# A fused attention and FP4 feed-forward block on one core: last batch's scaling moved to VectorE, ten unread matmul pairs fewer, another order of work

## The chip, the core and the metric

The kernel runs on one core of a Trainium2 chip. The time is device microseconds of one execution. The core has four compute engines, each of which works through its own instructions in the order in which they are written: PE (TensorE, matmuls and transposes), DVE (VectorE), ACT (ScalarE) and POOL (GpSimd). SP (SyncE) issues DMAs, and so does ACT. Engines wait for each other through semaphores.

## What is computed

For x of 8 batches x 512 rows x 128 columns, with xn = layernorm(x), the result is x + attention(xn) + ffn(xn):

```
qkv = xn @ w_qkv.T; q, k: 16 heads x 2 codes through fc_code; q = softmax over the codes
k_exp = exp(k - max over t); kv = cumsum(k_exp * v) / (cumsum(k_exp) + 1e-9)
attention = (sum over codes of q * kv) @ w_out.T

fp4(a): blocks of 16: scale = max|a| / 6, a / scale to the nearest of
        0, .5, 1, 1.5, 2, 3, 4, 6 (with sign), times scale
gate = fp4(xn) @ fp4(w_gate).T; up = fp4(xn) @ fp4(w_up).T      (352 columns each)
h = silu(gate) * up
ffn = fp4(h) @ fp4(w_down).T
```

All products are in fp32.

## The kernel before

A batch is 128 partitions x 4 tiles of 128 columns (a partition holds rows 4p to 4p+3, one in each tile). For each batch, the names in the code follow the work:

- DVE takes statistics (`stats`), ACT forms `xn`; PE transposes it (`xn_t` after ACT's copy) and multiplies by `wqkv_t` into `at_ps`. ACT copies `q_rel` and `v_sb`. DVE takes `k_max`, PE transposes it, DVE forms `k_negmax`, PE adds it, ACT writes the exponent into `kv`.
- POOL multiplies `kv<-v_sb,kv` (128x1024) and adds tile to tile (three `kv<-kv`, 128x288). PE sums over the partitions (`at_ps<-kv,before`), ACT adds the exponent of q (`at_ps<-q_rel`), DVE forms `kv<-kv,at_ps` (128x1152) and `den`, ACT its logarithm and exponent, DVE `den_p`, `den_r`, `q_n`. POOL forms `o_codes`, PE transposes and sums the codes, ACT copies `o_t`.
- fp4 of xn: DVE block maxima (`x_abs`, `x_max`, `x_recip`), ACT `x_r`, POOL `yx` = xn / scale, ACT squares its coarse part into PSUM (`s_ps<-yx`), DVE two operations (`sx`, `qx`) that leave the grid value, POOL `xq` = grid value times scale; PE transposes into `g_ps`, ACT copies `xq_t`.
- PE forms gates (`g_ps`, `h_ps`) and ups (`u_ps`), ACT the SiLU (`silu`), DVE `h`, `h_max`, `h_recip`, ACT `h_r`, POOL `yh`, ACT `s_ps<-yh` for a tile, DVE `sh` and `qh` (bf16, in SBUF), POOL `hq` = qh times h_max. PE transposes `hq`, ACT copies `hq_t`, PE sums the output product (`wo_t`) and the down products (`wd_t`) in `o_ps`, DVE adds x into `out_sb`, SP stores it.

There is one `s_ps` bank for yx and the four yh tiles, so that a new square waits for the DVE operation that read the last one. ACT needs two tables a batch, one with exponent and logarithm and one with SiLU, and loads each for 1.28 us.

The order on each engine is written out by hand: each engine's function is a loop over steps in which each piece of work stands under its own offset (`b = step - 55`) or fixed step, and the pieces of one step run in the order in which they are written. Batch 0 and batch 7 have pieces of their own. In batch 7, the four tiles of h go singly: POOL `yh` at L583, L357, L505, L386, DVE `sh` and `qh`, POOL `hq` at L362 (tile 0), L568 (1), L475 (3), L519 (2), and the output products in four banks (`o_ps`, `h_ps`, and both halves of `at_ps`) with one add each (L1098, L1406, L1400, L1208).

Among PE's work are 30 unread pairs: `o_ps<-before,ident`, two products of two constants that nobody reads.

## Time and profile before

| | us |
|---|---|
| median of 3 runs | 137.80 |
| lowest, highest | 137.77, 138.46 |
| the profiled execution | 137.86 |
| its span, from the first to the last instruction | 136.0 |
| PE, DVE, ACT, POOL busy in it | 129.3, 120.2, 114.4, 119.7 |

A row of a timeline gives the start and duration of an instruction, its engine and line, what it writes and reads, and, in brackets, how long its engine sat idle before it and what ended that. Durations overlap the next start by about 0.1 us, so sums go from start to start. Matmul ends are modelled. A row of windows gives the stretch, its length, for PE, its weight loads (PEld), DVE, ACT and POOL the busy time and (x count), then the granted clock of PE (1.00 is 2.4 GHz), the DMA share and GB/s.

### The profile page before, as it was taken

How to read it: one execution, taken by the hardware profiler on the slowest of the kernel's cores; microseconds unless marked ns; L12 is line 12 of the kernel's file. 1: busy time of each engine (PE TensorE's matmuls, PEld its weight loads, DVE VectorE, ACT ScalarE, POOL GpSimd, SP SyncE). 2: the span in 40 equal slices, each digit the busy share in tenths (PEclk: the TensorE clock that was granted, in tenths of full speed). 3: DMA queues.
4: the chain of work that ended last, by engine and by line, in shares of the span. 5: the costliest groups of instructions: out<-in, count | busy, mean ns of one | idle time of the engine just before them, and what ended most of it. 6: DMA issues, size and time to landing. Idle time of an engine off the chain costs nothing.

```text
span 136.0 us, 2542 instructions
## 1 busy us (share of the span) xinstructions
PE 129.3 (95%) x861; PEld 110.2 (81%) x861; DVE 120.2 (88%) x289; ACT 114.4 (84%) x280; POOL 119.7 (88%) x122
## 2 busy tenths in 40 slices
PE   2989999999999999999999999999999999978992
PEld 2979886888798878987898889788978895857992
DVE  1589999989999899989998999899989897999831
ACT  0778999979998999999899989998999778785640
POOL 5439889699999999999999999999999999999920
PEclk9999999999999999999999999999999999999999
DMA  4991000000000001000100020002000100010012
GB/s 104 317 367 65 5 2 0 2 0 2 0 5 0 0 0 77 5 0 0 77 0 5 2 80 0 0 0 82 0 0 0 77 0 0 5 77 0 6 71 77
DMA packets 4075, 5.14 MB, mean 38 GB/s; under 512 B 544, under 2 KB 2144, under 8 KB 4064
## 3 DMA queue, kind: packets, MB, share of 16 engines
q1 hardware_dynamic: 3088, 4.49, 9.4%
q10 hardware_dynamic: 976, 0.51, 1.3%
q8 instruction: 6, 0.10, 0.3%
q14 instruction: 5, 0.04, 0.1%
HBM read 2.90 MB, written 2.10 MB: 37 GB/s over the span
## 4 chain that ended last, share of the span: by engine, by line
PE 34%; ACT 21%; DVE 19%; POOL 19%; issue 4%; POOLq 0%; ACTq 0%
ACT L1025 4%; POOL o_codes L494 3%; DVE h_max L1358 2%; POOL hq L404 2%; POOL hq L529 2%; POOL yh L467 2%; PE at_ps L2040 2%; DVE h_max L1103 2%; ACT s_ps L1021 2%; ACT xn_t L922 2%; POOL kv L397 1%; POOL kv L449 1%; DVE sh L1300 1%; ACT silu L1025 1%; DVE x_abs L1174 1%
## 5 line engine op out<-in xcount | busy, mean ns | idle before, releaser
L494 POOL TENSOR_TENSOR o_codes<-kv,q_n 128x1024 f32<-128x1024 f32 x6 | 11.8, 1972 | 0.0
L449 POOL TENSOR_TENSOR kv<-v_sb,kv 128x1024 f32<-128x1024 f32 x6 | 11.8, 1969 | 0.0
L664 ACT ACTIVATE xn<-x_all,shift,rstd 128x128 f32<-128x128 f32 x24 | 9.9, 489 | 0.0
L2040 PEld LDWEIGHTS at_ps<-wqkv_t,xn_t 128*128 128x128 f32 x48 | 8.1, 190 | 1.3
L404 POOL TENSOR_TENSOR hq<-qh,h_max 128x704 f32<-128x704 bf16 x6 | 8.3, 1385 | 0.9 <-DVE qh L1363 0.9
L2040 PE MATMUL at_ps<-wqkv_t,xn_t 128*128 128x192 f32 x48 | 8.8, 326 | 0.0
L378 POOL TENSOR_TENSOR yh<-h,h_r 128x704 f32<-128x704 f32 x6 | 8.3, 1388 | 0.3 <-ACT h_r L793 0.3
L467 POOL TENSOR_TENSOR yh<-h,h_r 128x704 f32<-128x704 f32 x6 | 8.3, 1386 | 0.0
L529 POOL TENSOR_TENSOR hq<-qh,h_max 128x704 f32<-128x704 bf16 x6 | 8.3, 1383 | 0.0
L1392 DVE TENSOR_TENSOR kv<-kv,at_ps 128x1152 f32<-128x1152 f32 x6 | 8.1, 1344 | 0.0
L726 ACT ACT_TABLE_LOAD x6 | 7.7, 1283 | 0.1
L1025 ACT ACT_TABLE_LOAD x6 | 7.7, 1283 | 0.1
L442 POOL TENSOR_TENSOR yx<-xn,x_r 128x512 f32<-128x512 f32 x6 | 6.4, 1060 | 0.3 <-ACT x_r L846 0.3
L537 POOL TENSOR_TENSOR xq<-qx,x_max 128x512 f32<-128x512 bf16 x6 | 6.3, 1054 | 0.0
L1738 PE MATMUL at_ps<-ident,o_codes 128*128 128x128 f32 x24 | 5.6, 273 | 0.0
L1739 PE MATMUL at_ps<-ident,o_codes 128*128 128x128 f32 x24 | 5.6, 273 | 0.0
L1103 DVE TENSOR_REDUCE h_max<-h 128x44 f32<-128x748 f32 x6 | 5.5, 922 | 0.0
L1358 DVE TENSOR_REDUCE h_max<-h 128x44 f32<-128x748 f32 x6 | 5.5, 922 | 0.0
L810 ACT ACTIVATE o_t<-at_ps 128x512 f32<-128x512 f32 x6 | 3.6, 598 | 2.1 <-PE at_ps L1739 2.1
L367 POOL TENSOR_TENSOR kv<-kv 128x288 f32<-128x288 f32 x6 | 4.8, 801 | 0.3
L2163 PE MATMUL o_ps<-wd_t,hq_t 128*128 128x128 f32 x36 | 5.0, 275 | 0.0
L1903 PE MATMUL o_ps<-wd_t,hq_t 128*128 128x128 f32 x36 | 5.0, 275 | 0.0
(517 smaller groups left out, 525.7 us busy)
## 6 DMA issues: line engine op xcount, KB each, us to landing
x_all<-x SPq DMA_DIRECT2D x8, 256.0 KB, 4.9
out<-out_sb SPq DMA_DIRECT2D x7, 256.0 KB, 2.0
out<-out_sb SPq DMA_DIRECT2D x2, 128.0 KB, 1.7
w_raw<-w_down ACTq DMA_DIRECT2D x1, 176.0 KB, 4.8
wqk_raw<-w_qkv ACTq DMA_DIRECT2D x1, 128.0 KB, 3.5
w_raw<-w_gate SPq DMA_DIRECT2D x1, 128.0 KB, 3.2
w_raw<-w_up ACTq DMA_DIRECT2D x1, 128.0 KB, 3.5
wqkv_t<-w_qkv ACTq DMA_DIRECT2D x1, 64.0 KB, 4.3
```

The lines of the kernel that those rows point to most:

```text
L378: nc.gpsimd.tensor_tensor(blocks(yh[:, p, 0 * FF:2 * FF], PAIR * HB), h[:, p, 0 * HB:2 * HB, 0:BLOCK], spread(h_r[:, p, 0 * HB:2 * HB], PA ...
L404: nc.gpsimd.tensor_tensor(hq[:, 4 * p + 2:4 * p + 4, 0:FF].rearrange("p t (b k) -> p t b k", k=BLOCK), qh[:, p, 2 * FF:4 * FF].rearrange(" ...
L449: nc.gpsimd.tensor_tensor(kv[:, p, :, 0:KV].rearrange("p j (c h w) -> p j c h w", c=CODE, w=HEAD), v_sb[:, p, :].rearrange("p (j h w) -> p ...
L467: nc.gpsimd.tensor_tensor(blocks(yh[:, p, 2 * FF:4 * FF], PAIR * HB), h[:, p, 2 * HB:4 * HB, 0:BLOCK], spread(h_r[:, p, 2 * HB:4 * HB], PA ...
L494: nc.gpsimd.tensor_tensor(o_codes[:, p, :, :].rearrange("p j (c w) -> p j c w", w=HEAD), kv[:, p, :, 0:KV].rearrange("p j (c w) -> p j c w ...
L529: nc.gpsimd.tensor_tensor(hq[:, 4 * p + 0:4 * p + 2, 0:FF].rearrange("p t (b k) -> p t b k", k=BLOCK), qh[:, p, 0 * FF:2 * FF].rearrange(" ...
L664: last = nc.scalar.activation(xn[:, p, j * D:(j + 1) * D], x_all[:, b, j * D:(j + 1) * D], ACT.Identity, bias=shift[:, b, j:j + 1], scale= ...
L1025: nc.scalar.activation(silu[:, 1, :], h_ps[:, 0:FF], ACT.Silu).then_inc(silu1_done, 1)
L1103: nc.vector.tensor_reduce(h_max[:, p, 0 * HB:2 * HB], h[:, p, 0 * HB:2 * HB, :], AX.X, ALU.max, apply_absolute_value=True).then_inc(hmax0_ ...
L1358: nc.vector.tensor_reduce(h_max[:, p, 2 * HB:4 * HB], h[:, p, 2 * HB:4 * HB, :], AX.X, ALU.max, apply_absolute_value=True).then_inc(hmax1_ ...
L1392: nc.vector.tensor_tensor(kv[:, p, :, :], kv[:, p, :, :], a_ps[:, 0:ROW].unsqueeze(1).broadcast_to([P, TILES, ROW]), ALU.add).then_inc(bad ...
L2040: last = nc.tensor.matmul(at_ps[:, j // 2, j % 2 * QKV:(j % 2 + 1) * QKV], xn_t[:, p, j * P:(j + 1) * P], wqkv_t[:, :], start=(j % 2 == 0) ...
```

## The change

It changes six things.

1. hq of the last batch. The second rounding step writes the grid value as fp32 back into the PSUM bank from which it read instead of bf16 into `qh`, and DVE multiplies from there into `hq`. Tiles 1, 2 and 3 of that batch use the banks `g_ps`, `u_ps0` and `u_ps1` instead of `s_ps`. Four POOL instructions are gone. Batch 0's and the middle batches' hq stay on POOL, two tiles at a time.
2. Unread pairs: 20 instead of 30.
3. Loads: both pieces of w_up head ACT's queue (one was third there, one fourth on SP's), w_down is before the value weights.
4. The last batch is stored in four DMAs of one tile, in the order 0, 3, 1, 2, rather than two.
5. In the last batch PE starts the output product (`wo_t`) of each tile in a piece of its own.
6. All engines' pieces stand under other steps and in another order, and some waits change with it.

```diff
 sp (loads)
-            sp.dma_start(w_raw[0:FF - 2 * P, FFP + 2 * P:2 * FFP], w_up[2 * P:FF, :]).then_inc(gu_in, 16)
 act (loads, as they now stand)
+            act.dma_start(w_raw[:, FFP:FFP + 2 * P].rearrange("p (c k) -> p c k", c=2),
+                          w_up[0:2 * P, :].rearrange("(c p) k -> p c k", p=P)).then_inc(gu_in, 16)
+            act.dma_start(w_raw[0:FF - 2 * P, FFP + 2 * P:2 * FFP], w_up[2 * P:FF, :]).then_inc(gu_in, 16)
             act.dma_start(code_sb[:, :], code_t).then_inc(codes_in, 16)
             act.dma_start(wqk_raw[:, :, :], w_qkv[0:2 * D, :].rearrange("(s p) k -> p s k", p=P)).then_inc(codes_in, 16)
             act.dma_start(w_raw[:, 2 * FFP:], w_down).then_inc(down_in, 16)
             act.dma_start(wqkv_t[:, 2 * HC:], w_qkv[2 * D:3 * D, :]).then_inc(wv_in, 16)
 pool (one of four, all for b = BATCHES - 1)
-                    nc.gpsimd.tensor_tensor(blocks(hq[:, 4 * p + 0, 0:FF], HB), blocks(qh[:, p, 0 * FF:1 * FF], HB), spread(h_max[:, p, 0 * HB:1 * HB], HB), ALU.mult).then_inc(hq0_done, 1)
 dve (tile 0; the other tiles alike, from g_ps, u_ps0, u_ps1)
+                    nc.vector.scalar_tensor_tensor(out=s_ps[:, 0:FF], in0=s_ps[:, 0:FF], scalar=OFFSET, in1=sh[:, p, 0 * FF:1 * FF], op0=ALU.add, op1=ALU.subtract).then_inc(qh0_done, 1)
+                    dve.wait_ge(qh0_done, 8)
+                    nc.vector.tensor_tensor(blocks(hq[:, 4 * p + 0, 0:FF], HB), blocks(s_ps[:, 0:FF], HB), spread(h_max[:, p, 0 * HB:1 * HB], HB), ALU.mult).then_inc(hqz0_done, 1)
 act (tile 2; tiles 1 and 3 alike)
+                    nc.scalar.activation(u_ps[0][:, 0:FF], coarse(yh[:, p, 2 * FF:3 * FF]), ACT.Square, scale=SLOPE).then_inc(sqh2_done, 1)
 pe (ten of thirty such pieces are gone)
-                    for _ in range(2):
-                        nc.tensor.matmul(o_ps[:, 0:P], ident[:, :], before[:, :], start=True, stop=True)
 pe (last batch, tile 0; before, one piece)
+                    pe.wait_ge(ot_done, 8)
+                    pe.wait_ge(resid_done, 7)
+                    nc.tensor.matmul(o_ps[:, 0 * P:1 * P], o_t[:, p, 0 * P:1 * P], wo_t[:, :], start=True, stop=False).then_inc(woz0_done, 1)
 sp (last batch)
-            for half in range(2):
-                for ready in ((residz0_done, residz1_done), (residz2_done, residz3_done))[half]:
-                    sp.wait_ge(ready, 1)
-                sp.dma_start(out_v[b][:, half * 2 * P:(half + 1) * 2 * P], out_sb[:, b % 2, half * 2 * P:(half + 1) * 2 * P]).then_inc(last_stored, 16)
+            for j, ready in ((0, residz0_done), (3, residz3_done), (1, residz1_done), (2, residz2_done)):
+                sp.wait_ge(ready, 1)
+                sp.dma_start(out_v[b][:, j * P:(j + 1) * P], out_sb[:, b % 2, j * P:(j + 1) * P]).then_inc(last_stored, 16)
```

PE in the opening, around the transposes of xn of batch 2 (`at_ps<-ident,xn`), before. The rows of `o_ps<-before,ident` are unread pairs.

```order
L1706 MATMUL h_ps<-ident,w_dq 128x128 x3
L1710 MATMUL o_ps<-before,ident 128x128 x2
L1724 MATMUL g_ps<-ident,xq 128x128 x4
L1814 MATMUL at_ps<-kv,before 128x288
L1824 MATMUL o_ps<-before,ident 128x128 x2
L1827 MATMUL o_ps<-before,ident 128x128 x2
L1830 MATMUL o_ps<-before,ident 128x128 x2
L1833 MATMUL o_ps<-before,ident 128x128 x2
L1911 MATMUL at_ps<-ident,xn 128x128 x4
```

The same place now:

```order
L2144 MATMUL g_ps<-ident,xq 128x128 x4
L1706 MATMUL at_ps<-kv,before 128x288
L1740 MATMUL u_ps<-wu_t,xq_t 128x352
L1774 MATMUL h_ps<-ident,w_dq 128x128 x3
L1784 MATMUL at_ps<-ident,xn 128x128 x4
L1877 MATMUL u_ps<-wu_t,xq_t 128x352
L1890 MATMUL g_ps<-wg_t,xq_t 128x352
```

The four pairs ahead of the transposes are gone; an up product and the transposes of the down weights stand there.

DVE in a middle period, from x_abs to the large kv, before:

```order
L1174 TENSOR_REDUCE x_abs<-xn 128x32
L1202 TENSOR_REDUCE x_max<-x_abs 128x32
L1243 TENSOR_TENSOR h<-silu,u_ps 128x22x16
L1259 TENSOR_TENSOR h<-silu,u_ps 128x22x16
L1281 RECIPROCAL x_recip<-x_max 128x32
L1300 SCALAR_TENSOR_TENSOR sh<-s_ps,yh 128x352
L1358 TENSOR_REDUCE h_max<-h 128x44
L1363 SCALAR_TENSOR_TENSOR qh<-s_ps,sh 128x352
L1390 TENSOR_REDUCE at_ps<-at_ps 128x64
L1392 TENSOR_TENSOR kv<-kv,at_ps 128x1152
```

Now, with `out_sb` of the batch before among them (it was ahead of the first row, or behind it, before):

```order
L1447 TENSOR_REDUCE x_abs<-xn 128x32
L1490 TENSOR_TENSOR h<-silu,u_ps 128x22x16
L1515 SCALAR_TENSOR_TENSOR sh<-s_ps,yh 128x352
L1551 TENSOR_TENSOR out_sb<-x_all,o_ps 128x512
L1556 SCALAR_TENSOR_TENSOR qh<-s_ps,sh 128x352
L1562 TENSOR_REDUCE x_max<-x_abs 128x32
L1597 TENSOR_TENSOR h<-silu,u_ps 128x22x16
L1607 RECIPROCAL x_recip<-x_max 128x32
L1617 TENSOR_REDUCE h_max<-h 128x44
L1080 TENSOR_REDUCE at_ps<-at_ps 128x64
L1099 TENSOR_TENSOR kv<-kv,at_ps 128x1152
```

sh and qh moved ahead of the second h and of h_max.

DVE at the end, from the last batch's q_n to the last hq, before:

```order
L1588 SCALAR_TENSOR_TENSOR q_n<-at_ps,den_r 128x128
L1591 SCALAR_TENSOR_TENSOR sh<-s_ps,yh 128x352
L1606 TENSOR_TENSOR h<-silu,u_ps 128x22x16
L1620 SCALAR_TENSOR_TENSOR qh<-s_ps,sh 128x352
L1622 TENSOR_REDUCE h_max<-h 128x22
L1624 RECIPROCAL h_recip<-h_max 128x22
L1071 SCALAR_TENSOR_TENSOR sh<-s_ps,yh 128x352
L1088 SCALAR_TENSOR_TENSOR qh<-s_ps,sh 128x352
L1184 TENSOR_TENSOR out_sb<-x_all,o_ps 128x512
L1131 SCALAR_TENSOR_TENSOR sh<-s_ps,yh 128x352
L1352 SCALAR_TENSOR_TENSOR qh<-s_ps,sh 128x352
```

Now, from the first round in place on:

```order
L1197 SCALAR_TENSOR_TENSOR s_ps<-s_ps,sh 128x352
L1255 SCALAR_TENSOR_TENSOR sh<-u_ps,yh 128x352
L1291 RECIPROCAL h_recip<-h_max 128x22
L1352 TENSOR_TENSOR hq<-s_ps,h_max 128x352
L1437 SCALAR_TENSOR_TENSOR u_ps<-u_ps,sh 128x352
L1510 SCALAR_TENSOR_TENSOR sh<-g_ps,yh 128x352
L1520 TENSOR_TENSOR hq<-u_ps,h_max 128x352
L1530 TENSOR_TENSOR out_sb<-x_all,o_ps 128x512
L1612 SCALAR_TENSOR_TENSOR g_ps<-g_ps,sh 128x352
L1381 SCALAR_TENSOR_TENSOR sh<-u_ps,yh 128x352
L1456 TENSOR_TENSOR hq<-g_ps,h_max 128x352
L1466 SCALAR_TENSOR_TENSOR u_ps<-u_ps,sh 128x352
```

One product more (tile 2) follows. POOL's four products are gone, and its last instruction is yh of tile 2, behind o_codes.

## Rows read from the trace of the kernel before

**Rows 1.** The page: busy time of each engine, and TensorE's clock by slices.

```profile
PE 129.3 (95%) x861; PEld 110.2 (81%) x861; DVE 120.2 (88%) x289; ACT 114.4 (84%) x280; POOL 119.7 (88%) x122
...
PEclk9999999999999999999999999999999999999999
```

**Rows 2.** Windows of one period: length, busy time of each engine, clock, DMA share.

```profile
73.91:82.39 8.48, 8.48 (x60) 7.20 (x59) 8.48 (x21) 7.97 (x21) 8.25 (x9) 1.00 0.09 33
82.39:87.77 5.38, 5.38 (x35) 4.54 (x34) 4.91 (x13) 5.30 (x12) 5.38 (x4) 1.00 0.00 0
sum 13.86, PE 13.86 PEld 11.74 DVE 13.38 ACT 13.27 POOL 13.63; mean PE 6.93 PEld 5.87 DVE 6.69 ACT 6.63 POOL 6.81
```

**Rows 3.** Timeline of DVE in that period: start, duration, engine, line, operation.

```profile
84.74 0.53 DVE L1462 SCALAR_TENSOR_TENSOR qh<-s_ps,sh 128x352 bf16<-128x352 f32 x1
...
87.77 0.52 DVE L1561 TENSOR_TENSOR h<-silu,u_ps 128x352 f32<-128x352 f32 x1 [0.34 <-ACT silu L1025]
```

**Rows 4.** Timeline of ACT in that period.

```profile
85.98 1.28 ACT L1025 ACT_TABLE_LOAD   x1
87.27 0.46 ACT L1025 ACTIVATE silu<-h_ps 128x352 f32<-128x352 f32 x1
```

**Rows 5.** Timeline of PE in the opening: three unread pairs, batch 2's transposes.

```profile
2.44 1.22 PE L1642 MATMUL o_ps<-before,ident 128*128 128x128 f32 x4 [2.44 <-POOL head_of L348]
...
6.34 0.61 PE L1669 MATMUL o_ps<-before,ident 128*128 128x128 f32 x4
...
26.54 0.61 PE L1824 MATMUL o_ps<-before,ident 128*128 128x128 f32 x4
...
28.32 0.60 PE L1911 MATMUL at_ps<-ident,xn 128*128 128x128 f32 x4
```

**Rows 6.** Timeline of ACT in the opening.

```profile
6.55 1.65 ACT L633 ACTIVATE xn<-x_all,shift,rstd 128x128 f32<-128x128 f32 x4 [0.38 <-POOL shift L430]
8.79 0.24 ACT L705 ACTIVATE w_r<-w_recip 128x48 f32<-128x48 f32 x1 [0.60 <-DVE w_recip L1177]
...
28.96 0.60 ACT L922 ACTIVATE xn_t<-at_ps 128x512 f32<-128x512 f32 x1 [0.66 <-PE at_ps L1911]
```

**Rows 7.** Timeline of DVE in the opening.

```profile
6.03 0.95 DVE L1515 TENSOR_REDUCE w_abs<-w_raw 128x48 f32<-128x768 f32 x1 [1.04 <-DMA w_raw<-w_up]
...
30.23 0.29 DVE L1466 TENSOR_TENSOR den_p<-at_ps,den 128x128 f32<-128x128 f32 x1 [0.46 <-ACT at_ps L967]
...
32.52 0.52 DVE L1561 TENSOR_TENSOR h<-silu,u_ps 128x352 f32<-128x352 f32 x1
...
38.64 0.53 DVE L1273 SCALAR_TENSOR_TENSOR sh<-s_ps,yh 128x352 f32<-128x352 f32 x1 [0.26 <-ACT s_ps L762]
...
46.13 0.52 DVE L1561 TENSOR_TENSOR h<-silu,u_ps 128x352 f32<-128x352 f32 x1 [0.33 <-ACT silu L1025]
```

**Rows 8.** Timeline of DVE from the last steady period to q_n of the last batch.

```profile
101.76 0.52 DVE L1561 TENSOR_TENSOR h<-silu,u_ps 128x352 f32<-128x352 f32 x1 [0.27 <-ACT silu L1025]
...
120.86 1.34 DVE L1385 TENSOR_TENSOR kv<-kv,at_ps 128x1152 f32<-128x1152 f32 x1
...
124.16 0.29 DVE L1588 SCALAR_TENSOR_TENSOR q_n<-at_ps,den_r 128x128 f32<-128x128 f32 x1
```

**Rows 9.** Timeline of POOL at the end.

```profile
123.98 0.78 POOL L362 TENSOR_TENSOR hq<-qh,h_max 128x352 f32<-128x352 bf16 x1
...
124.72 1.97 POOL L573 TENSOR_TENSOR o_codes<-kv,q_n 128x1024 f32<-128x1024 f32 x1
```

**Rows 10.** Timeline of all engines over the last operations.

```profile
129.88 0.78 POOL L519 TENSOR_TENSOR hq<-qh,h_max 128x352 f32<-128x352 bf16 x1 [0.95 <-DVE qh L1352]
...
133.53 0.29 DVE L1208 TENSOR_TENSOR out_sb<-x_all,at_ps 128x128 f32<-128x128 f32 x1 [0.60 <-PE at_ps L1755]
```

**Rows 11.** The page's DMA issues: size, us from issue to landing.

```profile
out<-out_sb SPq DMA_DIRECT2D x7, 256.0 KB, 2.0
out<-out_sb SPq DMA_DIRECT2D x2, 128.0 KB, 1.7
```

## What the change does to the time

> **What bounds the kernel now.** I read the busy row of the page first: TensorE, ScalarE, VectorE and GpSimd are all busy 84% to 95% of a 136.0 us span [rows 1], so no share names the limit. The timelines of the four engines show three parts: an opening (to 46.13, where VectorE forms the first h of batch 2), a steady part of four periods (46.13 to 101.76), and an end (to 133.82, the last add on VectorE). One period runs 13.86 us, during which VectorE is busy 13.38, ScalarE 13.27, GpSimd 13.63, TensorE all of it [rows 2].
>
> What sets the period is a loop of two engines. From h L1561 (73.91) to kv L1392 (82.39) VectorE is busy 8.48 of 8.48 us. From kv it goes through h_recip, den, sh to qh L1462 at 84.74 [rows 2, 3]; then ScalarE may write the square of the next yx into s_ps (0.6), loads the SiLU table (85.98, 1.28) and forms silu (87.27, 0.46), for which VectorE waits 0.34 us at 87.77 [rows 3, 4]. 8.48 + 5.38 = 13.86. GpSimd and TensorE have only 0.2 us of slack each and follow.
>
> In the opening, TensorE never rests: unread pairs (ident times before, written to o_ps and never read) fill it. Four stand ahead of the transposes of batch 2's xn: 26.54 to 28.32, 1.78 us [rows 5]. ScalarE waits 0.66 for those transposes (xn_t at 28.96) [rows 6], den_log and its exponent come behind xn_t on ScalarE, VectorE waits 0.46 for them at den_p, and the next h comes at 32.52 [rows 7]. In the end, batch 7's four hq tiles are scaled on GpSimd, the last at 129.88 after a wait of 0.95 for VectorE's qh; from there transposes, copy, product and add run to 133.82 [rows 9, 10].
>
> **The change, part by part.** The diff's name speaks of the first and last batch; the orders show the four GpSimd products moved for the last batch only (batch 0 keeps its two double ones). So I count one batch.
>
> Opening, first weights. w_abs waits for w_up until 6.03 [rows 7]. Both w_up pieces now head ScalarE's queue and the last piece needed is w_gate's second, one issue (0.5 us) ahead of the old last one, so I take 5.5. w_recip no longer stands behind w_down's maxima, so w_r comes near 7.0 rather than 8.79 [rows 6]. But xn of batch 0, four activations of 1.65 us that began at 6.55, now stands behind w_r: 0.6 later, while the codes' four small activations stand behind xn. Behind the weights VectorE gets free earlier by 0.4 to 0.7. Six issues instead of five on ScalarE put its first table load 0.45 later, which ends before the statistics' results are missed by more than 0.1. I let these cancel: zero, between +0.6 and -0.7.
>
> Opening, pairs. Of 30 unread pairs 20 remain, and the four ahead of batch 2's transposes and one behind are gone. Where they stood TensorE has an up product, batch w_down's transposes: 0.59 + 0.33. The 0.66 that ScalarE waited goes, and the den chain, the s_ps write, the table load and h of batch 1 all move by it: 32.52 becomes about 31.9. The next period has the same VectorE work with one wait of 0.26 at sh L1273 [rows 7], which goes because that write of s_ps no longer follows the k exponent closely, and about 0.1 in small gaps. So h of batch 2 comes at 46.13 - 1.0 = 45.1. Bounds: 0.2 (another engine, GpSimd with its 2 us k-v product ahead of yx, becomes late) and 1.7 (the first batch's SiLU work, which I place 2 us earlier, carries through).
>
> Four periods. VectorE's instructions between kv and the next h are the same ones in the same order, and between h and kv the same set in another order (out_sb and one sh move behind the first of the two h, h_max last). So the loop's two pieces remain 8.48 and 5.38. Walking the new order by the durations of the period, the third s_ps write, now ahead of the exp table load, is ready 0.2 us before VectorE wants it, the exponent of q for at_ps 0.6 before, and GpSimd ends its list 0.3 before the next release. 4 x 13.86 = 55.44 against 55.63 measured (46.13 to 101.76; the last of the four had 13.99) [rows 7, 8]: -0.2. Bounds -1.0 (down to the roughly 13.65 that TensorE's issue times add up to) and +2 (a half microsecond per period).
>
> Turn to the last batch, 101.76 to q_n's end at 124.45 [rows 8], 22.7 us. GpSimd has kv's last prefix adds ahead of hq and of the big o_codes of batch 6 instead of behind it, 1.93 earlier in its list, and ScalarE's table load comes sooner. VectorE's list between is the same but for h of tile 2 (0.43), which goes ahead of q_n in place of the last round of tile 0 (0.43), which goes behind. By VectorE's sum the second kv comes 18.6 us after the h rather than 19.1 [rows 8], q_n with it: -0.5, between 0 and -1.0. GpSimd would be ready for o_codes by then because hq of tile 0 (0.78, 123.98) no longer stands before it (124.72) [rows 9].
>
> Last stretch, q_n's end to the last add's end: 9.37 now. VectorE now has behind q_n: h_max 0.45, four rounds, three sh and four products, eleven at about 0.43 start to start, a reciprocal 0.2, out_sb 0.6, together 6.0 us; with 0.3 for operations that follow their own input directly, the last hq ends 6.3 after q_n. On that last path stand then transposes 0.5, copy 0.5, three products 0.9 and add 0.3, with handovers 2.4: 8.7, so -0.7. The GpSimd product of 0.78 with its handovers on the old path is what goes. The in-place round in PSUM and the product read from PSUM into hq do not exist in the trace. Lower bound: the 0.43 of every 352-column VectorE operation that reads PSUM; upper: the 0.78 of the same product on GpSimd [rows 9, 10], which times four plus four gives 2.8 us more. I take 0.43, since the operand count and shape are those of qh at 84.74 (0.53 with its overlap) [rows 3], and keep -1.2 to +1.5 for the term.
>
> Stores. Four of 64 KB instead of two of 128; the last still starts after the last add, and landing took 1.7 us for 128 KB against 2.0 for 256 KB [rows 11]. I take 0, between -0.2 and +0.4 (the third issue, about 0.4, still running). The Trainium skill, DMA: Bandwidth & Descriptors, section on where the time of a DMA goes, has a fixed part of about 2 us plus bytes over 436 GB/s; by it the halves would save about 0.15 us, an estimate that the sum doesn't hold.
>
> Sum: -1.0 - 0.2 - 0.5 - 0.7 = -2.4. The profiled execution took 137.86 us, its span of 136.0 and 1.86 around it; the median of the runs shown is 137.8, so I predict **135.4**.
>
> **Rivals.**
> 1. The opening's gain is lost: GpSimd's or ScalarE's new order in the first 30 us replaces the removed wait. For it: xn held behind w_r, and yx of batch 1 now behind the 1.97 us k-v product. Then only 1.2 remains: 136.6.
> 2. The periods shrink to about 13.65: TensorE's and GpSimd's own work. For it, the relief of ScalarE ahead of its table load; against, the write of s_ps still waits for the same qh. 135.4 - 1.0 = 134.4.
> 3. VectorE becomes the bound of the end: each of the eight new or changed PSUM operations costs 0.15 more, or out_sb of batch 6 holds o_ps's product: 136.6.
> 4. Slower: ScalarE misses a date in every period. The s_ps write (0.4) that moved ahead of the exp table load delays the k exponent, the prefix sum on TensorE, the q exponent and so VectorE's kv. With the 0.6 of slack that I find, a delay of 1.0 us makes each period 0.4 longer, and six of them eat the 2.4: the point from which it decides. At 1.1 the price is 6 x 0.5 = 3.0 and the result 138.4.
> 5. The clock. The first pair took 1.22 us, that at 6.34 0.61, four matmuls each [rows 5]; the page's clock row reads 9, its highest, in all 40 slices, the end included, where TensorE waits several times [rows 1]. Fewer pairs leave gaps near 11 and 14 us; I count none over 0.8 us. Ten microseconds of opening at half the clock would cost about 3 with TensorE as the bound: 138.5.
>
> For the last the Trainium skill (TensorE: Matmul & The Clock Gate, the table of what to do) warns of idle gaps between bursts of matmuls and would have the clock fall to 1.2 GHz, which speaks against taking pairs out. What it would give here is rival 5's time.
>
> **How the numbers follow.** Forecast 0.52 (its own range 134.7 to 136.3), rival 1 0.14, rival 2 0.11, rival 3 0.09, rival 4 0.08, rival 5 0.03, and 0.03 for gains and losses that cancel. The range 134.0 to 137.0 reaches the first three rivals and leaves out the slower ones. A change of 0.5% (0.7 us) is about what a measurement of this kernel can tell from none. Faster by more: forecast and rivals 1 to 3 with most of their spread, 0.84; within, 0.08; slower, 0.08.
>
> **What would show it.** h L1309 of batch 2 near 45.1 with no wait of ScalarE for xn's transposes; periods of 13.86 with VectorE full between h L1309 and kv L1099; the second kv of the end 18.6 after batch 6's h; 352-column operations in PSUM of 0.52 us, 0.43 apart; GpSimd idle after about 126; 2.1 to 2.3 us from the last add to the end. Periods over 14.2, a clock below 1.00 in the first 40 us, or PSUM products of 0.7 would prove me wrong.

## The result and the profile after

| | before | after |
|---|---|---|
| median, us (10 runs each, same chip) | 138.09 | 136.86 |
| lowest, highest | 137.23, 139.85 | 136.46, 137.55 |
| ratio of the times, 95% interval | | 0.9923 [0.9897, 0.9949] |
| the profiled execution, its span | 137.86, 136.0 | 136.56, 134.5 |

The change makes the kernel 1.2 us faster (0.8%). Forecast were 2.4 us and 135.4. Before's median is 0.3 above that of the three runs which the prediction started from, so the time missed by 1.5 us and the difference by 1.2. The range and the sign held. In all tables the medians are of all runs, and the ratios leave out those in a slower state, more than 1.5% above the fastest run of the same kernel.

The page of the kernel after; the first line answers to [rows 1], the other to [rows 11] (size, median us from issue to landing):

```profile
PE 125.9 (94%) x821; PEld 106.4 (79%) x821; DVE 121.8 (91%) x293; ACT 114.0 (85%) x280; POOL 116.5 (87%) x118
...
out<-out_sb SPq DMA_DIRECT2D x4, 64.0 KB, 1.6
```

VectorE timeline of after, opening; answers to [rows 7] (line numbers are those of the new kernel):

```profile
4.89 0.95 DVE L1144 TENSOR_REDUCE w_abs<-w_raw 128x48 f32<-128x768 f32 x1 [0.47 <-DMA w_raw<-w_gate]
...
8.39 0.77 DVE L1338 BATCH_NORM_STATS2 stats<-x_all 128x6 f32<-128x256 f32 x2 [0.37 <-DMA x_all<-x]
...
10.94 0.54 DVE L1342 SCALAR_TENSOR_TENSOR w_s<-g_ps,w_y 128x384 f32<-128x384 f32 x1
...
20.26 0.52 DVE L1222 TENSOR_TENSOR h<-silu,u_ps 128x352 f32<-128x352 f32 x1 [0.25 <-PE u_ps L1815]
...
24.48 0.69 DVE L1447 TENSOR_REDUCE x_abs<-xn 128x32 f32<-128x512 f32 x1 [0.55 <-ACT xn L653]
...
30.61 0.29 DVE L1250 TENSOR_TENSOR den_p<-at_ps,den 128x128 f32<-128x128 f32 x1 [0.25 <-ACT at_ps L990]
...
32.90 0.52 DVE L1309 TENSOR_TENSOR h<-silu,u_ps 128x352 f32<-128x352 f32 x1 [0.28 <-ACT silu L1044]
...
46.02 0.52 DVE L1309 TENSOR_TENSOR h<-silu,u_ps 128x352 f32<-128x352 f32 x1 [0.30 <-ACT silu L1044]
```

w_abs comes 1.14 earlier than in [rows 7], yet h of batch 1 comes at 32.90, 0.38 later. (A second profile of the same kernel, e0_changed_again below, has it at 33.58, so the profile after is an early one.) ScalarE's rows, against [rows 6]: w_r comes 2.1 earlier; the wait for batch 2's transposes ahead of xn_t is gone, but xn_t itself is no earlier, and the wait now stands at den_log:

```profile
6.66 0.24 ACT L721 ACTIVATE w_r<-w_recip 128x48 f32<-128x48 f32 x1 [1.27 <-DVE w_recip L1294]
...
29.06 0.59 ACT L949 ACTIVATE xn_t<-at_ps 128x512 f32<-128x512 f32 x1
...
29.95 0.31 ACT L966 ACTIVATE den_log<-den 128x128 f32<-128x128 f32 x1 [0.30 <-DVE den L1165]
```

Windows of the same period as in [rows 2]: stretch, length, busy time (and count) of PE, PEld, DVE, ACT, POOL, clock, DMA share, GB/s.

```profile
73.59:81.98 8.39, 8.39 (x60) 7.12 (x59) 8.39 (x21) 8.02 (x21) 8.15 (x8) 1.00 0.09 33
81.98:87.35 5.37, 5.37 (x35) 4.57 (x34) 4.90 (x13) 5.31 (x12) 5.37 (x5) 1.00 0.01 3
```

VectorE from the last steady period to the end; answers to [rows 8] and [rows 10]:

```profile
101.05 0.52 DVE L1309 TENSOR_TENSOR h<-silu,u_ps 128x352 f32<-128x352 f32 x1 [0.28 <-ACT silu L1044]
...
120.27 1.34 DVE L1585 TENSOR_TENSOR kv<-kv,at_ps 128x1152 f32<-128x1152 f32 x1
...
123.44 0.29 DVE L1104 SCALAR_TENSOR_TENSOR q_n<-at_ps,den_r 128x128 f32<-128x128 f32 x1
...
128.28 0.51 DVE L1456 TENSOR_TENSOR hq<-g_ps,h_max 128x352 f32<-128x352 f32 x1
128.71 0.52 DVE L1466 SCALAR_TENSOR_TENSOR u_ps<-u_ps,sh 128x352 f32<-128x352 f32 x1
129.27 0.53 DVE L1622 TENSOR_TENSOR hq<-u_ps,h_max 128x352 f32<-128x352 f32 x1
...
132.14 0.29 DVE L1366 TENSOR_TENSOR out_sb<-x_all,at_ps 128x128 f32<-128x128 f32 x1 [0.38 <-PE at_ps L2151]
```

Start to start, the two executions compare so:

| stretch | before | after | difference | forecast |
|---|---|---|---|---|
| start to h of batch 1 | 32.52 | 32.90 | +0.38 | -0.6 |
| to h of batch 2 | 13.61 | 13.12 | -0.49 | -0.4 |
| four periods | 55.63 | 55.03 | -0.60 | -0.2 |
| h of batch 6 to q_n's end | 22.69 | 22.68 | -0.01 | -0.5 |
| q_n's end to the last add's end | 9.37 | 8.70 | -0.67 | -0.7 |
| last add to the span's end | 2.18 | 2.07 | -0.11 | 0 |
| sum, the span | 136.0 | 134.5 | -1.50 | -2.4 |

The time fell by 1.30, since what lies around the span was 2.06 instead of 1.86.

### The profile page after: what moved, and what is told of

It is laid out like the page before. It is cut to its first block, busy times and chain, and to the rows that moved or that the text cites. A ratio compares the mean times of both kernels' runs of the same rounds, so it can differ in the third digit from the quotient of the medians.

```text
span 134.5 us, 2464 instructions
## 1 busy us (share of the span) xinstructions
PE 125.9 (94%) x821; PEld 106.4 (79%) x821; DVE 121.8 (91%) x293; ACT 114.0 (85%) x280; POOL 116.5 (87%) x118
## 4 chain that ended last, share of the span: by engine, by line
PE 78%; ACT 10%; DVE 4%; POOL 4%; issue 2%; POOLq 0%
PE at_ps L1910 5%; PE o_ps L2131 3%; PE o_ps L2115 3%; PE o_ps L1951 3%; PE o_ps L1842 2%; PE u_ps L2136 2%; ACT xn L653 2%; PE u_ps L1877 2%; PE u_ps L2021 2%; PE h_ps L2056 2%; PE h_ps L1901 2%; PE g_ps L2032 2%; PE g_ps L1890 2%; PE at_ps L1696 2%; PE at_ps L1719 2%; PE at_ps L1720 2%
## 5 line engine op out<-in xcount | busy, mean ns | idle before, releaser
L2115 PE MATMUL o_ps<-wd_t,hq_t 128*128 128x128 f32 x36 | 5.0, 275 | 0.0
L1842 PE MATMUL o_ps<-wd_t,hq_t 128*128 128x128 f32 x36 | 5.0, 275 | 0.0
L1951 PE MATMUL o_ps<-wd_t,hq_t 128*128 128x128 f32 x36 | 5.0, 275 | 0.0
L2131 PE MATMUL o_ps<-wd_t,hq_t 128*128 128x128 f32 x36 | 5.0, 275 | 0.0
```

What stands on the lines that cost most here:

```text
L1951: last = nc.tensor.matmul(o_ps[:, 0 * P:1 * P], hq_t[:, 0, c * P:(c + 1) * P], wd_t[:, c * P:(c + 1) * P], start=False, stop=(c == CHUNKS ...
L2115: last = nc.tensor.matmul(o_ps[:, 2 * P:3 * P], hq_t[:, 2, c * P:(c + 1) * P], wd_t[:, c * P:(c + 1) * P], start=False, stop=(c == CHUNKS ...
L2131: last = nc.tensor.matmul(o_ps[:, 3 * P:4 * P], hq_t[:, 3, c * P:(c + 1) * P], wd_t[:, c * P:(c + 1) * P], start=False, stop=(c == CHUNKS ...
```

## The experiments

"h1" is the start of h of batch 1 on VectorE, "w_s" that of the first w_s (rounding of the gate and up weights). Each ratio is against runs of before on the same chip, whose median there was 138.1 to 138.6. Each profile had a granted clock of 1.00, but for e1_pool_swap's. The numbers w_s, h1 and span are of one execution each.

| run | median (lowest to highest) | ratio [95%] | w_s | h1 | w_s to h1 | span |
|---|---|---|---|---|---|---|
| before | 138.09 (137.23, 139.85) | | 11.69 | 32.52 | 20.83 | 136.0 |
| after | 136.86 (136.46, 137.55) | .9923 [.9897, .9949] | 10.94 | 32.90 | 21.96 | 134.5 |
| e1_pool_swap | 136.88 | .9858 [.9777, .9938] | | | | |
| e2_xpath | 136.49 (136.34, 136.86) | .9845 [.9777, .9913] | 10.74 | 32.71 | 21.97 | 134.3 |
| e4_qkv_path | 136.94 (136.92, 137.04) | .9875 [.9809, .9941] | 11.40 | 33.26 | 21.86 | 134.9 |
| e5_both | 136.86 (136.32, 136.98) | .987 [.9791, .995] | 10.75 | 32.65 | 21.90 | 134.3 |
| e3_before_4pairs_out | 137.78 (137.39, 138.41) | .9943 [.9907, .9978] | 11.60 | 32.27 | 20.67 | 135.6 |
| e6_loads_as_before | 137.57 (136.91, 139.73) | .9939 [.9898, .9981] | 12.61 | 34.66 | 22.05 | 136.3 |
| e7_both_2pairs_out | 137.17 (136.71, 137.62) | .988 [.98, .9959] | 12.07 | 33.97 | 21.90 | 135.6 |
| e8_hq_on_gpsimd | 137.81 (137.18, 138.36) | .9935 [.9903, .9967] | 11.21 | 33.18 | 21.97 | 135.5 |
| e12_hq_two_each | 137.31 (136.74, 139.07) | .9913 [.9881, .9945] | 11.54 | 33.49 | 21.95 | 135.1 |
| e14_hmax_order | 138.46 (137.87, 138.99) | 1.0003 [.9976, 1.0029] | 11.27 | 33.24 | 21.97 | 136.4 |
| e9a_attention0_first | 137.16 (136.91, 137.71) | .9923 [.9894, .9951] | 11.46 | 33.41 | 21.95 | 135.0 |
| e9_attention01_first | 137.77 (137.0, 139.3) | .9973 [.9939, 1.0007] | 10.99 | 33.36 | 22.37 | 134.9 |
| e0_changed_again | 137.06 (136.81, 137.45) | .9898 [.9871, .9925] | 11.62 | 33.58 | 21.96 | 135.2 |
| e2r_xpath_again | 136.92 (136.3, 137.09) | .9876 [.9844, .9907] | 11.32 | 33.29 | 21.97 | 134.9 |
| e16_xn0_in_the_wait | 136.72 (136.4, 136.88) | .9869 [.9844, .9895] | 11.35 | 33.31 | 21.96 | 134.9 |
| e17a_codes_behind_wy | 137.21 (136.47, 137.84) | .992 [.9887, .9952] | 11.57 | 33.52 | 21.95 | 135.1 |
| e17_codes_and_xpath | 136.98 (136.68, 137.55) | .9916 [.9887, .9946] | 11.12 | 33.29 | 22.17 | 134.9 |
| e18_batch2_stats_later | 136.82 (136.62, 137.37) | .9884 [.984, .9928] | 11.55 | 33.50 | 21.95 | 135.1 |

Two columns tell most of the story. In the changed kernel and in all versions of it w_s to h1 is 21.86 to 22.37, in 13 of 17 profiles 21.90 to 21.97, against 20.83 before; and span less h1 is 101.5 to 101.7 wherever the end and the periods were left alone. So a profile's span is that of its first w_s plus a constant, and no reordering that I made between w_s and h1 shortened that stretch by more than 0.10.

### The opening: what holds h of batch 1

**GpSimd's order.** First suspicion: yx of batch 1 behind the 1.97 us product of k and v. Changed kernel, yx put ahead of it:

```diff
 pool (yx of the middle batches)
-                if 1 <= b < BATCHES - 1:
+                if 2 <= b < BATCHES - 1:
 pool (ahead of kv<-v_sb,kv of batch 0)
+                    b = 1
+                    pool.wait_ge(xr_done, b + 1)
+                    nc.gpsimd.tensor_tensor(blocks(yx[:, p, :], TILES * XB), blocks(xn[:, p, :], TILES * XB), spread(x_r[:, p, :], TILES * XB), ALU.mult).then_inc(yx_done, 1)
```

> The changed kernel with one edit: on GpSimd, yx of batch 1 stands ahead of the k-v product of batch 0 instead of behind it. Theory A (GpSimd's order lost the opening: 1.97 us of k-v product ahead of yx): yx starts about 17.8 instead of 19.68, ScalarE's wait of 0.36 goes, h of batch 1 comes at 32.3 to 32.5 instead of 32.90, time 136.4. Theory B (x_r of batch 1 only ends at 19.57, because VectorE takes x_abs of batch 1 behind two statistics and ScalarE x_r behind the table load): yx still starts at 19.6, GpSimd waits for it, the k-v product comes at 20.6 instead of 17.76 and all that follows on GpSimd up to 2.9 later less the slack; h of batch 1 33.0 to 34.0, time 137.0 to 137.9.

The profiled execution ran at a granted clock of 0.86 and took 149.5 us, so only the order of its early events is read. GpSimd's timeline:

```profile
20.32 1.06 POOL L501 TENSOR_TENSOR yx<-xn,x_r 128x512 f32<-128x512 f32 x1 [2.28 <-ACT x_r L852]
```

GpSimd stands idle before yx for x_r of ScalarE, so it isn't the product that holds yx. Its other three executions took 136.4 to 136.9, as the changed kernel: the theory fell.

**The two paths of batch 1.** e2 puts x_abs, x_max and x_recip of batch 1 ahead of two statistics on VectorE, x_r ahead of ScalarE's table load and yx ahead of the product; e4 puts the transposes, xn_t, its product, q_rel and v_sb of batch 1 earlier; e5 does both.

```diff
 dve (e2; ahead of the statistics of two later batches)
+                    b = 1
+                    dve.wait_ge(xn_done, b + 1)
+                    nc.vector.tensor_reduce(x_abs[:, :, 0], blocks(xn[:, p, :], TILES * XB), AX.X, ALU.max, apply_absolute_value=True).then_inc(xabs_done, 1)
...
 act (e2; ahead of the silu of batch 0)
+                    nc.scalar.activation(x_r[:, p, :], x_recip[:, p, :], ACT.Copy, scale=GRID_MAX / SHADE).then_inc(xr_done, 1)
 pe (e4; the transposes of batch 1, in place of an unread pair, and two waits for the silu)
-                if 1 <= b < BATCHES - 1:
+                if 2 <= b < BATCHES - 1:
...
+                    pe.wait_ge(silu1_done, 1)
...
+                        pe.wait_ge(silu2_done, 1)
```

> The changed kernel with batch 1's fp4 path put as in the kernel before: on VectorE x_abs, x_max and x_recip ahead of the two statistics at 16.25 and 16.92, on ScalarE x_r ahead of the SiLU table load, on GpSimd yx ahead of the k-v product. Theory B: yx starts at 17.8, the wait of 0.36 before s_ps<-yx goes, xn of batch 2 and the exp table load come 0.4 earlier, h of batch 1 at 32.5, time 136.4. Theory C (the order on TensorE binds: q_rel waits for the product of batch 1's xn_t, L1910 at 20.65, whatever yx does): the 0.36 comes back as a longer wait before q_rel (0.4 becomes about 0.8), xn of batch 2 stays at 22.8, h of batch 1 at 32.8 to 33.0, time 136.8 to 137.0.

> The changed kernel with batch 1's attention path earlier: on TensorE the transposes of xn ahead of the up and gate products of batch 0 and the xn_t product ahead of gate 2 of batch 0, on ScalarE xn_t ahead of the second silu, q_rel and v_sb ahead of the third; two waits of TensorE for a silu that this order needs. Theory C: the wait of 0.40 before q_rel goes, q_rel starts at 21.4 and xn of batch 2 at 22.4 instead of 22.81, exp table load 24.5, h of batch 1 at 32.5, time 136.4. Theory B (yx alone binds, s_ps<-yx at 20.77 stays): xn of batch 2 within 0.15 of 22.8, h of batch 1 at 32.8 to 33.0.

> The edits of the two kernels before this one together (batch 1's fp4 path and its attention path earlier). If both waits of ScalarE, 0.36 and 0.40, made the loss: xn of batch 2 at 22.0 to 22.2, exp table load at 24.2 to 24.3, the large kv of batch 1 at 27.2, h of batch 1 at 32.2, time 136.1. If VectorE's or GpSimd's own work takes over (theory D: the statistics moved behind and the k-v product 1.0 later make the prefix sum or x_recip late), h of batch 1 stays at 32.8 or later although both waits are gone.

In e2 yx of batch 1 starts at 17.70 instead of 19.68, and the wait of 0.36 for it is gone, but ScalarE then waits 0.84 instead of 0.40 at q_rel, and w_s to h1 is the same 21.97. In e4, where ScalarE still waits 0.36 and 0.34, it is 21.86, in e5, with one wait of 0.81 at q_rel, 21.90: 0.1 at most. None of the three differs from the changed kernel by more than the intervals leave open.

**Unread pairs.** Before with only the four pairs of step 70 taken out:

```diff
 pe (before; four such pieces)
-                if step == 70:
-                    for _ in range(2):
-                        nc.tensor.matmul(o_ps[:, 0:P], ident[:, :], before[:, :], start=True, stop=True)
```

> The kernel before with one edit: the four unread pairs ahead of the transposes of batch 2's xn are gone (L1824 to L1833). The prediction's step: ScalarE's wait of 0.66 before xn_t goes whole, h of batch 1 at 31.9 instead of 32.52, and all after it 0.6 earlier: time 0.6 less than before. Rival (the cap): den on VectorE ends at 29.33 whatever TensorE does, den_log started at 29.58, so only 0.2 can be gained: ScalarE now waits 0.2 to 0.4 before den_log for den, h of batch 1 at 32.3, time 0.2 less than before. Rival (clock): the gap of 1.8 us brings TensorE's clock down, 1 us or more slower.

VectorE's timeline of it, against [rows 7], and then a row of ScalarE's:

```profile
27.25 1.34 DVE L1347 TENSOR_TENSOR kv<-kv,at_ps 128x1152 f32<-128x1152 f32 x1
...
29.98 0.29 DVE L1466 TENSOR_TENSOR den_p<-at_ps,den 128x128 f32<-128x128 f32 x1 [0.25 <-ACT at_ps L967]
...
32.27 0.52 DVE L1561 TENSOR_TENSOR h<-silu,u_ps 128x352 f32<-128x352 f32 x1
```

```profile
29.32 0.31 ACT L956 ACTIVATE den_log<-den 128x128 f32<-128x128 f32 x1 [0.46 <-DVE den L1440]
```

The four pairs delayed den_p by 0.25 (30.23 before), not by the 0.66 that ScalarE waited: behind the transposes the next late thing is `den`, which VectorE itself ends at 29.3 and for which ScalarE now waits 0.46 before its logarithm. VectorE's wait at den_p fell from 0.46 to 0.25 and stays there. From kv to h is 5.02, as in after (27.88 to 32.90), and 5.22 before: 0.20 of the 0.25 arise there, the other 0.05 stood already at kv. The time (137.78, 0.57 under before's) allows for a little more, with the next interval 0.17 shorter too (h of batch 2 at 45.71).

Whether the pairs that are left hold something was asked by taking two more out of e5:

```diff
 pe (the pairs that stand at L1893 and L1828 in the changed kernel)
-                    for _ in range(2):
-                        nc.tensor.matmul(o_ps[:, 0:P], ident[:, :], before[:, :], start=True, stop=True)
```

> The changed kernel with batch 1's fp4 and attention paths earlier, as in e5_both, and two unread pairs gone (L1893, L1828, one on each side of the transposes of xq of batch 0), 18 left. Theory F (TensorE is the bound from 15.5 to 22.1 and its unread pairs stand on the path): the first gate product 0.4 earlier (16.75), ScalarE's wait before q_rel 0.4 instead of 0.81, h of batch 1 at 32.2 to 32.3 instead of 32.65, time 0.4 less than e5_both. Theory E (the sum of ScalarE's work is the bound): the gain at q_rel is lost again by xn of batch 2, h of batch 1 within 0.1 of 32.65.

w_s to h1 is 21.90, exactly e5's. TensorE now waits 0.36 for xq, so these two pairs held nothing; ahead of the product of batch 2's xn_t it waits 1.61, and in the changed kernel 1.62 (32.07). ScalarE still waits 0.81 at q_rel for TensorE's product of batch 1's xn_t, so TensorE as a whole isn't cleared by this.

**Loads.** The changed kernel with before's order of loads:

```diff
 sp
+            sp.dma_start(w_raw[0:FF - 2 * P, FFP + 2 * P:2 * FFP], w_up[2 * P:FF, :]).then_inc(gu_in, 16)
 act (the first of the two loads of w_up is back behind wqk_raw, w_down behind wqkv_t)
-            act.dma_start(w_raw[0:FF - 2 * P, FFP + 2 * P:2 * FFP], w_up[2 * P:FF, :]).then_inc(gu_in, 16)
```

> The changed kernel with the loads issued as in the kernel before (second piece of w_up fourth on SP, the first third on ScalarE's queue, five issues on ScalarE). If the early weights carry the opening now: w_abs at 6.0 instead of 4.89, w_r at 7.8 instead of 6.66 with xn of batch 0 behind it, h of batch 0 at 20.6 instead of 19.49, h of batch 1 0.8 to 1.1 later, time 137.7. If they are worth nothing (the rest of the opening is bound by ScalarE's own work, which here starts 0.5 earlier): h of batch 1 within 0.3 of 32.9, time 136.9.

```profile
7.16 0.95 DVE L1144 TENSOR_REDUCE w_abs<-w_raw 128x48 f32<-128x768 f32 x1 [2.62 <-DMA w_raw<-w_up]
...
12.61 0.54 DVE L1342 SCALAR_TENSOR_TENSOR w_s<-g_ps,w_y 128x384 f32<-128x384 f32 x1
```

With before's order of loads w_s is 1.0 to 1.7 later than in the two profiles of the changed kernel, and the median is 0.5 to 0.7 higher. How much of that is the loads is less sure: in this execution w_abs waited for w_up until 7.16, 1.1 later than in before (6.03) with the same order of loads, the runs were on other chips, and by the ratios, whose intervals overlap, it is 0.2 to 0.6 us. The sign fits the first theory; my sum had put the term at nothing.

**Attention of batches 0 and 1 forward**, to fill ScalarE's waits ahead of its table loads (e9a: batch 0, e9: both; three and four unread pairs fewer):

```diff
 act (e9a; the k exponent of batch 0, until now behind the copies of the weights, ahead of wg_t; xn_t, q_rel, v_sb alike)
+                    act.wait_ge(kshift_done, 1)
...
                     act.wait_ge(wT_done, 1)
                     nc.scalar.activation(wg_t[:, :], h_ps[:, 0:FF], ACT.Copy, scale=GRID_MAX ** -2).then_inc(wev_done, 1)
 pe (e9a; the product that shifts k, and the transpose of k_max, earlier; three pairs out)
-                        nc.tensor.matmul(o_ps[:, 0:P], ident[:, :], before[:, :], start=True, stop=True)
```

> The changed kernel with batch 0's attention path put forward: three unread pairs ahead of xn's transposes gone (17 left), ScalarE's xn_t, q_rel and v_sb of batch 0 ahead of what filled the time before them, k_max and k_negmax earlier on VectorE, their products earlier on TensorE, the k exponent ahead of wg_t, the k-v product of batch 0 ahead of w_dq of the down weights. Theory H (the order of batch 0's attention path lost the opening): the k exponent of batch 0 at 15.7 instead of 17.40, but batch 1's path stands where it did, so h of batch 1 gains only what ScalarE no longer waits (0.2 to 0.4): 32.5 to 32.7. Theory D (GpSimd and VectorE pay for it: w_dq of the down weights, rstd and shift 1.9 later): h of batch 1 at 33 or later.

> The same, and batch 1's fp4 and attention paths follow it ahead of batch 0's SiLU work: x_abs, x_max, x_recip ahead of w_s of the down weights, x_r, xn_t of batch 1 ahead of the SiLU table load, TensorE's transposes and product of batch 1's xn ahead of the up products of batch 0, q_rel and v_sb ahead of the second silu; 16 unread pairs left. Theory E (what counts up to h of batch 1 is the sum of ScalarE's work and its waits, and all its waits behind 10 us, 1.7 us in the changed kernel, can be filled by this order): its waits between 10 and 32 fall to about 0.6, the exp table load of batch 1 at 24.0 instead of 24.94, h of batch 1 at 32.0 to 32.3, time 136.1. Theory F (TensorE's packed list between 15.5 and 22 is the bound): batch 0's gates and ups come 1.3 later, h of batch 1 at 32.9 or later.

ScalarE's timeline of e9:

```profile
24.79 0.24 ACT L674 ACTIVATE h_r<-h_recip 128x44 f32<-128x44 f32 x1 [0.79 <-DVE h_recip L1404]
```

The waits that were filled open again at h_r, which waits for VectorE. w_s to h1 became 22.37 in e9, and its time can't be told from before's; in e9a it stayed at 21.95. Neither moved h of batch 1 forward, so these theories fell as well.

**What starts it.** Two executions of the same program differed: w_s at 10.94 and at 11.62 (e0). e2 was run once more beside it (e2r).

> The changed kernel itself once more, on the chip of the two runs that follow, as their yardstick: 136.6 to 137.1; h of batch 1 at 32.7 to 33.2, since the loads of the opening land up to half a microsecond apart from one execution to the next.

> e2_xpath once more beside the changed kernel. If putting batch 1's fp4 path ahead is worth what its trace showed (h of batch 1 at 32.71 instead of 32.90): 0.2 less than the changed kernel. If its median of 136.5 was more than chance, 0.4 less. If nothing: the two medians within 0.1.

e2r is 0.14 under e0 in the median, with overlapping runs, so the low 136.49 of e2 did not come again. GpSimd's code_diff waits for wqk_raw, which now lands behind w_up, and w_y stands behind it: 7.30 in the one execution, 8.05 in the other, and h1 followed. Three runs took up what leads to w_y. e16 (on e2) has xn of batch 0 in ScalarE's wait for w_recip, xn_t of batch 0 earlier, three unread pairs out and a load moved to SP; e17a has code_diff behind w_y in the changed kernel, e17 the same in e2.

```diff
 pool (e17a, e17)
-                if step == 5:
+                if step == 7:
                     pool.wait_ge(codes_in, 2 * 16)
                     nc.gpsimd.tensor_tensor(code_diff[:, 0:1], code_sb[:, 1:2], code_sb[:, 0:1], ALU.subtract)
 act (e16; xn of batch 0, now ahead of w_r)
+                    act.wait_ge(shift_done, 1)
+                    for j in range(TILES):
+                        last = nc.scalar.activation(xn[:, p, j * D:(j + 1) * D], x_all[:, b, j * D:(j + 1) * D], ACT.Identity,
...
```

> e2_xpath, and ScalarE's wait of 1.27 for w_recip in the opening filled: the value weights' load issued on SP, so that ScalarE has five issues, xn of batch 0 ahead of w_r instead of behind it, three unread pairs ahead of xn's transposes gone (17 left), xn_t of batch 0 ahead of the first square of the weights. Theory E (ScalarE's work and waits up to h of batch 1 are the bound): xn at 6.0 to 6.2 and the wait gone, w_r at 7.8, the first square at 9.5 instead of 9.33 behind xn_t, the SiLU table load at 17.2 instead of 17.7, h of batch 1 at 32.2 to 32.3, time 0.4 less than e2_xpath. Theory W (the weights' own path, w_recip to w_r to w_y to w_dq to wg_t, carries the opening, and its 1.1 us of delay at w_r is what counts): the SiLU table load at 18.2 or later, h of batch 1 at 33.2 or later, time 0.5 or more above e2_xpath.

> The changed kernel with one edit on GpSimd: the two code_diff operations, which wait for the load of the q and k weights (wqk_raw), stand behind w_y of the gate and up weights instead of ahead of it. Theory W2 (w_up ahead of wqk_raw in the queue made GpSimd, not the weights, late: in twelve traces h of batch 1 comes 25.4 to 25.6 behind the start of w_y, and w_y starts when wqk_raw has landed, 0.4 to 1.5 behind w_r): w_y at 6.9 to 7.0 in every execution, h of batch 1 at 32.4 to 32.5, time 0.5 to 0.8 less than the changed kernel's 136.9 to 137.1. Rival (another wait takes its place: code_bd on ScalarE then waits for code_diff behind the 1.5 us of w_y, and the first square behind it): code_bd 0.3 or more later, the first square at 9.6 or later, h of batch 1 32.9 or later.

> The same edit on top of e2_xpath. Theory W2: h of batch 1 at 32.2 to 32.3, time 0.2 less than e17a_codes_behind_wy and 0.5 to 0.8 less than e2r_xpath_again's 136.9: 136.2. Rival as there: no gain over e2r_xpath_again.

In e16 w_r came at 7.76, 1.1 later than in after, and w_s to h1 stayed at 21.96 and the time at 136.72, so the time moved in neither of the ways expected; e17 gave no gain over e2r. VectorE's timeline of e17a:

```profile
7.47 0.76 DVE L1494 BATCH_NORM_STATS2 stats<-x_all 128x6 f32<-128x256 f32 x2 [0.62 <-DMA x_all<-x]
...
9.03 0.77 DVE L1338 BATCH_NORM_STATS2 stats<-x_all 128x6 f32<-128x256 f32 x2 [0.35 <-DMA x_all<-x]
```

w_y started at 7.21, earlier than in any other version with these loads but e2 and e5, and h1 still came at 33.52: w_y only came late together with what sets w_s. That is x. The statistics of batches 1 and 2 on VectorE wait for their loads, up to 0.97 and 0.42, ahead of the scales of w_down and of batch 0; with x on time they begin at 6.75 and 8.39, late at 7.5 and 9.1. From the statistics of batch 2 to the first w_s are 2.53 to 2.55 us in all profiles of the new order but e6 (2.78) and e18, and no row of VectorE in between shows a wait; in after the next is at 20.26.

**The last question** was whether VectorE's full list or the chain of batch 0's scales through x_r sets the start of what leads to h1.

```diff
 dve (statistics of batch 2, from ahead of x_abs of batch 0 to behind its x_recip)
+                if step == 2:
+                    dve.wait_ge(x_in[2], 16)
+                    for a in range(2):
+                        last = nc.vector.bn_stats(stats[:, 2, a, :], x_all[:, 2, a * 2 * D:(a + 1) * 2 * D].rearrange("p (two d) -> p d two", two=2))
+                    last.then_inc(stats_done, 1)
```

> The changed kernel with one thing moved on VectorE: the two statistics of batch 2 (0.68 from start to start, until now ahead of x_abs of batch 0, where they wait 0.35 to 0.37 for the load of x) stand behind x_recip of batch 0. Nothing is left out. In the profiles so far the statistics of batch 2 began at 8.39 (changed kernel) and 9.08 (its second profile), and h of batch 1 came 24.50 after them both times; the first x_r came at 10.77 and 11.45, and h of batch 1 came 22.13 after it both times. Theory V: from these statistics to 20.26 VectorE is packed, and its own list is the bound of the opening. Then the order inside it gives nothing, only the wait for x goes (0.37, and 0.4 of it comes back as a wait for xn ahead of x_abs): the first w_s stays at 10.9 to 11.1, sx at 12.8 to 13.0, h of batch 1 at 32.9 to 33.1, time 136.7 to 136.9. Theory R: the bound is the chain x_abs, x_max, x_recip, x_r, yx, s_ps of batch 0. Then x_abs begins at 8.5 to 8.7, x_r at 10.3 to 10.5, sx at 12.4 to 12.6, and h of batch 1 comes at 32.4 to 32.6; time 136.3 to 136.5. In both, a late load of x no longer moves h of batch 1.

x of batch 1 came later than ever (VectorE's timeline):

```profile
7.89 0.77 DVE L1494 BATCH_NORM_STATS2 stats<-x_all 128x6 f32<-128x256 f32 x2 [0.84 <-DMA x_all<-x]
...
11.55 0.54 DVE L1342 SCALAR_TENSOR_TENSOR w_s<-g_ps,w_y 128x384 f32<-128x384 f32 x1
...
33.50 0.52 DVE L1314 TENSOR_TENSOR h<-silu,u_ps 128x352 f32<-128x352 f32 x1 [0.28 <-ACT silu L1044]
```

x_r came at 10.90, from which the chain would give 33.03; w_s came at 11.55, from which 33.51 follows. h1 was 33.50: up to w_s VectorE's list decides. The absolute times of that theory (32.9 to 33.1) failed, because the order didn't free VectorE from batch 1's load, only from batch 2's, and "a late load no longer moves h" was wrong. The median of 136.82 is the changed kernel's.

What then makes w_s to h1 1.13 longer than before? The instructions of VectorE in it are the same, 48 by the windows. Windows of before, then of after, over that stretch (length, then PE, PEld, DVE, ACT, POOL):

```profile
11.69:32.52 20.83, 20.79 (x136) 17.58 (x136) 19.90 (x48) 19.49 (x56) 18.44 (x20) 1.00 0.01 2
```

```profile
10.94:32.90 21.96, 19.24 (x114) 15.27 (x113) 20.30 (x48) 20.06 (x55) 19.18 (x22) 1.00 0.01 2
```

VectorE's idle time is 1.66 instead of 0.93, its busy time 0.40 more. Three waits are new, in the rows of after above: 0.25 at 20.26 for u_ps of TensorE, 0.55 at 24.48 for xn of ScalarE, 0.28 at 32.90 for silu of ScalarE; one, at den_p, is 0.21 smaller. So from 20.26 on VectorE's list alone isn't the bound; three times it waits for others. The place of the loss can be read from its x_abs of batch 2, which waits for that xn: it starts 12.11 behind w_s in before, without a wait, and 13.54 in after, and from there to h1 after is 0.30 faster (8.42 against 8.72). ScalarE's rows narrow it down to the stretch between its two table loads. Its timeline of before:

```profile
19.20 1.28 ACT L1031 ACT_TABLE_LOAD   x1
...
24.32 1.28 ACT L726 ACT_TABLE_LOAD   x1
```

And of after:

```profile
17.70 1.28 ACT L826 ACT_TABLE_LOAD   x1
...
20.77 0.60 ACT L1040 ACTIVATE s_ps<-yx 128x512 f32<-128x512 bf16 x1 [0.36 <-POOL yx L439]
...
22.15 0.28 ACT L622 ACTIVATE q_rel<-at_ps 128x128 f32<-128x128 f32 x1 [0.40 <-PE at_ps L1910]
...
24.94 1.28 ACT L725 ACT_TABLE_LOAD   x1
```

The first load comes 1.50 earlier than before, the second 0.62 later: 7.24 us between them instead of 5.12. Then 7.96 instead of 8.20 lead to h1, and -1.50 + 2.12 - 0.24 is its +0.38. In before ScalarE does xn_t and the square of yx of batch 1 ahead of the first load, and q_rel, v_sb and xn behind two silus; now xn_t and the square stand between the loads, with the two waits of 0.36 and 0.40, and xn comes behind three silus. The stretch is 6.95 to 7.25 in every version at full clock; e2, e4, e5 and e9, whose edits work on it, shorten it by 0.3 at most. None put back before's order of ScalarE as a whole, so the place of the loss is shown, and which of these moves causes it is not.

### The four periods

Theory: it is VectorE's order that gains, sh and qh of the third tile now ahead of the second h and of h_max. In e14 they stand behind the second h and around h_max again in batches 1 to 5, as in before; ScalarE's wait ahead of its first square of h follows. out_sb is not put back ahead of the first h, as the expectation has it: it stands directly behind it, 0.4 earlier than in the changed kernel, since sh no longer stands between.

```diff
 dve (sh and qh of the third tile, b = 1 to 5: back behind the second h, and behind h_max)
-                if 1 <= b < BATCHES - 1:
+                if b == BATCHES - 2:
...
+                if 1 <= b < BATCHES - 2:
+                    dve.wait_ge(sqh2_done, b + 1)
+                    nc.vector.scalar_tensor_tensor(out=sh[:, p, 2 * FF:3 * FF], in0=s_ps[:, 0:FF], scalar=OFFSET, in1=yh[:, p, 2 * FF:3 * FF], op0=ALU.add, op1=ALU.subtract).then_inc(sh2_done, 1)
```

> The changed kernel with VectorE's order before kv in the middle batches put back: sh and qh of tile 2 behind the second h and around h_max, out_sb ahead of the first h. Theory L (VectorE's order alone made its piece from h to kv 8.39 instead of 8.48): the piece is 8.48 again, the period 13.86 instead of 13.76, time 0.5 more. Rival (the piece is the same, and ScalarE's or GpSimd's relief made the periods shorter): the piece stays 8.39 to 8.42, time within 0.2 of the changed kernel.

```profile
74.49 0.52 DVE L1309 TENSOR_TENSOR h<-silu,u_ps 128x352 f32<-128x352 f32 x1 [0.33 <-ACT silu L1044]
...
80.09 0.69 DVE L1530 TENSOR_TENSOR out_sb<-x_all,o_ps 128x512 f32<-128x512 f32 x1 [0.40 <-PE o_ps L2141]
...
83.36 1.35 DVE L1099 TENSOR_TENSOR kv<-kv,at_ps 128x1152 f32<-128x1152 f32 x1
```

h to kv takes 8.87, kv to h (88.74) 5.38 as ever. 0.40 of the 8.87 is a wait of out_sb, which now comes ahead of its data; the other 8.47 is before's 8.48. In the two of the four periods that show no wait the piece takes 8.61 and 8.60, against 8.39 to 8.42 in after. The periods are 14.14, 13.99, 14.25 and 13.96, 56.34 together against 55.03, and the whole gain of the change is gone. That is more than the 0.5 expected, because of the waits, but the rival, by which the piece stays, is out. So the loop of VectorE and ScalarE is the bound, and the order of VectorE's list inside it is worth 0.1 to 0.2 a period, and up to 0.4 more when one operand isn't ready.

### The end

Changed kernel with the four hq of the last batch back on GpSimd (banks, steps and all else kept; the rounding writes bf16 into qh again):

```diff
 pool (behind the last yh; tiles 3, 1 and 2 alike)
+                    pool.wait_ge(qh0_done, 8)
+                    nc.gpsimd.tensor_tensor(blocks(hq[:, 4 * p + 0, 0:FF], HB), blocks(qh[:, p, 0 * FF:1 * FF], HB), spread(h_max[:, p, 0 * HB:1 * HB], HB), ALU.mult).then_inc(hqz0_done, 1)
 dve (likewise)
-                    nc.vector.tensor_tensor(blocks(hq[:, 4 * p + 0, 0:FF], HB), blocks(s_ps[:, 0:FF], HB), spread(h_max[:, p, 0 * HB:1 * HB], HB), ALU.mult).then_inc(hqz0_done, 1)
```

> The changed kernel with only the scaling of the last batch undone: the second rounding writes bf16 into qh, and GpSimd forms the four hq products behind yh of tile 2 (126.5), in the order 0, 3, 1, 2; the squares keep the four banks of their own. The prediction's step (a product of 0.78 with its handovers on GpSimd costs the end 0.7 against 0.43 on VectorE): last hq ends at 130.4 or later instead of 129.80, last add 0.6 to 0.9 later, time 137.5. Rival Q (the banks of their own, not the engine, gave the 0.7): VectorE, free of three products, has the last round done at 127.5, GpSimd ends its four products back to back at 129.6, the last add comes within 0.2 of 132.1, time 136.8.

GpSimd's, TensorE's and VectorE's timelines of it:

```profile
126.77 0.79 POOL L462 TENSOR_TENSOR hq<-qh,h_max 128x352 f32<-128x352 bf16 x1
```

```profile
127.61 0.55 PE L2003 MATMUL h_ps<-ident,hq 128*128 128x128 f32 x3 [0.39 <-POOL hq L462]
```

```profile
133.17 0.29 DVE L1369 TENSOR_TENSOR out_sb<-x_all,at_ps 128x128 f32<-128x128 f32 x1 [0.38 <-PE at_ps L2139]
```

q_n's end to the last add's end is 9.43 against 8.70: 0.73 for the move. That stretch is 8.70 to 8.72 in every other version with the new order at full clock, and 9.37 and 9.38 in before and e3, so 0.73 is far outside its spread; the medians by themselves (ratios .9935 and .9923) would not show it. TensorE waits 0.39 for the first tile's hq and 0.20 for the second's. The last of the four started at 129.00 and ended at 129.79, which is 5.76 after q_n's end; in after it was 129.80, 6.07 after. So the last hq isn't what holds the end. The chain of work that ended last in the changed kernel (start, us, what) shows what is, TensorE's own list, which the chain follows back past 120 without a wait for any hq:

```profile
127.64 0.46 PE o_ps L2027 x2
...
130.22 0.33 PE u_ps L2045 x3
130.54 0.22 PE at_ps L1886 x2
130.77 0.67 PE at_ps L1733 x6
131.44 0.68 PE at_ps L2151 x6
...
132.14 0.29 DVE out_sb L1366
```

In before it was the same: the chain there is TensorE's own list from 125.10, where it waits for hq_t of batch 6, to the last add. The transposes of the last hq start at 131.38 with no wait, 0.7 behind its end at 130.66:

```profile
125.10 0.55 PE h_ps L2092 x3
...
131.38 0.33 PE u_ps L1937 x3
```

If that is so, only the first two tiles' hq need be on VectorE, early enough for TensorE not to wait. e12 has tiles 0 and 3 there, 1 and 2 on GpSimd:

> The changed kernel with the scaling of two tiles of the last batch on VectorE as now (0 and 3, the first two) and of the last two (1 and 2) on GpSimd behind its last yh. The prediction's step (the last hq sets the end, a product of 0.78 with its handovers stands on its path): the last add 0.3 to 0.7 later than in the changed kernel. Theory K (TensorE's list is packed from the wo products at 127.6 to the end, and what counts is when the first two tiles' hq let it start): the last stretch stays 8.7 within 0.1, time 136.9, although the last hq comes from GpSimd; with all four on GpSimd it was 9.4 with the last hq 0.3 earlier.

```profile
129.60 0.79 POOL L464 TENSOR_TENSOR hq<-qh,h_max 128x352 f32<-128x352 bf16 x1 [0.21 <-DVE qh L1465]
```

Its last hq ended at 130.39, 6.07 after q_n's end at 124.32, and the last add ended 8.71 after it: as after. So the first two of the four moved products carry the whole 0.7.

## Where the prediction was right and where wrong

- **What bounds the kernel.** Right for the periods (kv to h 5.37, h to kv packed, e14). Not for the opening: I named TensorE, which never rests there, while up to w_s it is VectorE's list behind the loads of x, and from 20.26 on VectorE also waits for others, 0.83 of 1.08 us for ScalarE. Not for the end either: I put the last hq on the path, and the chain of before passes it by.
- **First weights, zero.** Too small in size. w_abs at 4.89 (5.5 forecast) and w_r at 6.66 (7.0) were near. The first w_s came 0.75 earlier in the profile after but 0.07 earlier in its second profile, and e6 puts the loads at 0.2 to 0.7, not clear of the noise. I cancelled it against xn behind w_r; xn did start 0.25 later, but no row shows a wait for it.
- **Pairs, -0.6 on h of batch 1.** The step that failed. I carried ScalarE's wait of 0.66 straight to h without asking what is late next, though [rows 7] show VectorE waiting only 0.46 at den_p. Next was `den` of VectorE: the pairs alone are worth 0.25 on h1 (e3). The larger part of the miss is a term that the sum didn't have, the new order's 1.13 between w_s and h1, which stands between ScalarE's two table loads (7.24 us instead of 5.12). Rival 1 spoke of it and named ScalarE among its engines; its grounds (xn behind w_r, yx behind the product) were not the cause (e1, e2), and of ScalarE's moves none was singled out. Its 136.6 (136.4 by the sum without the opening's 1.0) was the nearest case, and its chance of 0.14 too low. The bounds of this term, a gain of 0.2 to 1.7 on h of batch 2, did not hold the 0.11 measured.
- **The period behind it, -0.4.** -0.49, right, and the wait at sh is gone as forecast; the pairs alone give 0.17 of it (e3).
- **Four periods, -0.2.** Right in the mechanism, too small: I held the two pieces at 8.48 and 5.38; the first became 8.39 to 8.42, and two of before's four periods had been longer than 13.86 by 0.06 and 0.13, so -0.60 came out. "The same set in another order costs the same" failed by 0.1 a period. Rival 2's 13.65 did not come (13.76), rival 4's lost dates neither.
- **Turn, -0.5.** Wrong. The second kv came 19.22 after h, where I had summed 18.6 and before's rows have 19.10. VectorE's list there is the same set, and moving h of tile 2 against a round can't shorten a full list. Up to the next h that waits for silu (0.63 in both) it is 12.38 in before and 12.37 in after, although before's wait of 0.42 for u_ps at 107.38 is gone: the silu came no sooner. No row of VectorE shows a wait that GpSimd's earlier prefix adds could have removed.
- **Last stretch, -0.7.** -0.67. The size was right, the path only half. The products in place took 0.51 to 0.53 us, 0.43 apart where independent and 0.56 where one follows its own input (128.71 to 129.27), the lower of my bounds. But my sum ran over the last hq (6.3 to its end and 2.4 behind it, measured 6.07 and 2.63), and its errors cancelled by luck. The end is set by TensorE's list and by whether the first two tiles' hq are there in time for it, not by the last hq (e8, e12). Nor did the banks of their own give the gain: e8 keeps them and loses it.
- **Stores, 0.** -0.11: 64 KB landed in 1.6, 128 KB in 1.7. The Trainium skill (DMA: Bandwidth & Descriptors, Anatomy of one DMA) would have given 0.15 less for the halves; the trace agrees within its rounding. Its fixed part of about 2 us, which it states for DMAs issued by GpSimd, is more than these stores of SyncE took altogether.
- **The clock, rival 5.** It didn't come. TensorE was busy 12.67 of the 13.12 between the h of batches 1 and 2, waited 1.62 in one piece for q_n ahead of 32.07, and every window shows 1.00. The warning of the Trainium skill (TensorE: Matmul & The Clock Gate, Why this matters for your kernels) against gaps between bursts had no case here.
- **The base.** The three runs of before had a median of 137.8; over 7 to 30 runs beside the experiments before's median was 138.1 to 138.6. That moves the time of the forecast, not its difference.

No version beats the changed kernel clearly. e2 (136.49, and 136.92 the second time) and e16 (136.72) have the lowest medians, and their intervals overlap the changed kernel's.

## What to carry to other kernels

A wait that an edit removes is worth the distance to the next thing that is late, not its own length: look up what else the waiting operation needs, and when that ends. Where one engine's list is full, moving work inside it gains only what its waits give back; before reading anything else, take the distance between two of its fixed points (here the first w_s and h of batch 1) in several profiles, since what is constant there is bound inside, though not always by that engine, and what varies comes from ahead. At an end with several parallel tiles, ask which tile the list of the last engine waits for; here it was not the last one.

## What the runs showed of the hardware

Loads of the opening vary between executions of one program. The statistics of batch 1 wait for x until 6.75 or less in after, and until 7.50 in its second profile, and the span went with it (134.5 and 135.2). From issue to landing the two pages have 4.8 and 5.6 us for x (median of eight) and 4.7 and 5.4 for wqk_raw, but 3.2 both times for w_up, which heads its queue.

TensorE's first pairs run at about half pace, 0.85 from start to start instead of 0.45, in before until 5.89 and in after, with the same unread pairs at that place, until 7.59 (its timeline):

```profile
6.87 0.89 PE L1665 MATMUL o_ps<-before,ident 128*128 128x128 f32 x4
7.59 0.61 PE L1668 MATMUL o_ps<-before,ident 128*128 128x128 f32 x4
```

The granted clock of the window from 2.40 to 7.60 is printed as 1.00 all the same, so that number did not tell the slow start. It ended between 5.8 and 8.4 in the profiles at full clock. Mostly unread pairs stood in it, and I take its cost for small; no run tests that.
